# Two root products in three fp32r terms and one weight slab split on VectorE, in a relational graph network

## What is computed

```python
def _rgcn(x, W_rel, W_root, bias, src, dst, etype):
    xr = jnp.einsum('ni,rio->rno', x, W_rel)
    msg = xr[etype, src]
    out = x @ W_root + bias
    for r in range(NUM_RELATIONS):
        m = etype == r
        s = jax.ops.segment_sum(jnp.where(m[:, None], msg, 0.0), dst, num_segments=n)
        c = jax.ops.segment_sum(m.astype(x.dtype), dst, num_segments=n)
        out = out + s / jnp.maximum(c, 1.0)[:, None]
    return out
```

## Time and profile before

| what | value |
|---|---|
| median of three runs | 878.64 us (878.55 to 879.24) |
| the profiled execution, its own time | 879.18 us |
| its span | 877.4 us |
| TensorE matmul busy | 803.3 us, 92% |
| VectorE busy | 604.2 us, 69% |
| ScalarE busy | 388.4 us, 44% |
| GpSimd busy | 502.6 us, 57% |
| mean granted TensorE clock | 0.972 |
| layer 0 about | 60 to 116 us |
| gate of layer 0 | 116 to 283 us |
| layer 1 about | 280 to 345 us |
| layers 2, 3 and 4 about | 516 to 590, 590 to 671, 671 to 755 us |
| attention networks | 755 to 877 us |

### The profile page before, as it was taken

One profiled execution on the slowest core, in us unless ns is written; L12 is line 12 of the kernel. 1 busy time (PEld: TensorE's weight loads), 2 busy tenths in 40 slices (PEclk: granted clock), 3 DMA queues, 4 the chain that ended last, 5 costly groups with the idle time before them and its releaser, 6 DMA issues.

```text
span 877.4 us, 10143 instructions
## 1 busy us (share of the span) xinstructions
PE 803.3 (92%) x4034; PEld 632.5 (72%) x4034; DVE 604.2 (69%) x671; ACT 388.4 (44%) x448; POOL 502.6 (57%) x214
## 2 busy tenths in 40 slices
PE   8999999999788999988997879999999998987987
PEld 3569976775455798666655459987997897864674
DVE  8955149999997622988999968534853888254451
ACT  1124366777663333766765524432342342241521
POOL 0346629999884472899998917661873478000000
PEclk9999999999999999999999989999999999979999
DMA  9036516254332452440533237633652653600000
GB/s 368 2 87 237 160 54 183 61 151 137 108 108 72 164 169 102 133 106 1 204 112 105 72 120 279 212 109 134 226 180 72 247 189 105 237 14 1 1 1 36
DMA packets 24262, 110.98 MB, mean 126 GB/s; under 512 B 3604, under 2 KB 5908, under 8 KB 23832
## 3 DMA queue, kind: packets, MB, share of 16 engines
q1 hardware_dynamic: 23096, 104.24, 36.3%
q10 hardware_dynamic: 1120, 6.10, 1.8%
HBM read 100.63 MB, written 0.79 MB: 116 GB/s over the span
## 4 chain that ended last, share of the span: by engine, by line
PE 61%; DVE 21%; POOL 12%; ACT 4%; issue 2%; DMA 0%; ACTq 0%; DVEq 0%
PE ps L958 22%; DVE prod L1679 12%; PE ps L906 11%; PE ps L943 6%; POOL prod L544 6%; POOL w_lo L532 4%; PE ps L1335 3%; DVE qi_t L1697 3%; PE ps L1195 2%; PE ps L1017 2%; POOL prod L547 2%; PE ps L1038 2%; PE ps L1148 2%; PE ps L1394 2%; PE ps L1320 1%
## 5 line engine op out<-in xcount | busy, mean ns | idle before, releaser
L532 POOL TENSOR_TENSOR w_lo<-w_raw,w_hi 128x1536 fp32r<-128x1536 f32 x54 | 201.5, 3742 | 148.6 <-ACT w_hi L598 148.5
L544 POOL TENSOR_TENSOR prod<-prod 128x1024 f32<-128x1024 f32 x94 | 223.5, 2400 | 49.1 <-DVE prod L1679 48.7
L705 ACT ACTIVATE prod<-ps 128x1024 f32<-128x1024 f32 x192 | 187.1, 1024 | 78.4 <-PE ps L1148 60.5
L1679 DVE TENSOR_TENSOR prod<-prod,ps 128x2048 f32<-128x2048 f32 x96 | 217.6, 2278 | 5.0 <-ACT prod L705 4.0
L1148 PE MATMUL ps<-sel_pair,h_and_q 128*128 128x512 f32 x384 | 129.7, 450 | 24.6 <-ACT prod L705 24.3
L906 PE MATMUL ps<-w_raw,h_t 128*128 128x384 f32 x408 | 141.7, 494 | 0.0
L598 ACT ACTIVATE w_hi<-w_raw 128x1536 fp32r<-128x1536 f32 x54 | 80.3, 1488 | 136.7 <-PE ps L958 92.9
L958 PE MATMUL ps<-w_hi,yt_hi 128*128 128x384 f32 x432 | 111.6, 339 | 8.1 <-POOL w_lo L532 8.1
L906 PEld LDWEIGHTS ps<-w_raw,h_t 128*128 128x128 f32 x408 | 78.7, 194 | 46.6 <-issue 2.6
L1148 PEld LDWEIGHTS ps<-sel_pair,h_and_q 128*128 128x128 f32 x384 | 67.2, 191 | 60.6 <-ACT prod L705 40.4
L958 PE MATMUL ps<-w_lo,yt_hi 128*128 128x384 f32 x432 | 110.4, 336 | 0.0
(11 more groups left out here) (189 smaller groups left out, 1001.8 us busy)
## 6 DMA issues: line engine op xcount, KB each, us to landing
w_raw<-weights SPq DMA_DIRECT2D x105, 768.0 KB, 4.4
wa_in<-weights SPq DMA_DIRECT2D x6, 768.0 KB, 5.8
w_gat<-weights SPq DMA_DIRECT2D x6, 768.0 KB, 8.0
w_query<-weights SPq DMA_DIRECT2D x3, 768.0 KB, 11.2
h_and_q<-stage_hi SPq DMA_DIRECT2D x24, 96.0 KB, 2.1
h_and_q<-stage_lo SPq DMA_DIRECT2D x24, 96.0 KB, 2.2
a_vec<-gat_vectors ACTq DMA_DIRECT2D x1, 2048.0 KB, 8.2
q_t<-queries ACTq DMA_DIRECT2D x1, 1536.0 KB, 10.6
```

The source lines that it names most:

```text
L532: pool.tensor_tensor(Wl[:, j, :], raw_slab(U, 0, j), Wh[:, j, :], ALU.subtract).then_inc(w_lo_ready, 1)
L544: pool.tensor_tensor(v[:, :, 0:32], v[:, :, 0:32], v[:, :, 32:64], ALU.add).then_inc(folded_once, 1)
L705: act.activation(slot_view(s)[:, :, 32 * u:32 * u + 32], args.rearrange("p b (n l) -> p (b n) l", l=LH), ACT.Sigmoid).then_inc(sigmoid_rea ...
L1679: TT(slot_view(s), slot_view(s), ps[:, 6, o:o + L].unsqueeze(1).broadcast_to([P, NB, L]), ALU.mult).then_inc(products_ready, 1)
```

## The change

Five edits, which come together:

1. Layers 3 and 4: the root is a split product in three terms. Its weight slabs get a high part from ScalarE and a low part from VectorE. The turned state is no longer kept in fp32: ScalarE writes its high part (`root_hi`) and VectorE its low part (`root_lo`) from PSUM. Both tiles' roots now run before the first aggregation.
2. All five layers: the low part of the last relation's third slab is written by VectorE, after `relation` of the last relation (in layers 2 to 4 after the `logit_weights` that follows it). GpSimd has the two other slabs and all slabs of the relations before; it has nothing for the roots.
3. Reciprocals of degrees of four types are computed in layer 2 and kept in `rinv4`; layers 3 and 4 compute none (8 fewer on VectorE).
4. ScalarE's list at the change of layer is written anew.
5. On VectorE `counts_of_all` goes from layer 4 to layer 3 (after relation 3), the wait for `vectors_in` behind relation 2 of layer 2, and of the last `logit_weights` the second half goes behind the norm of tile 0.

```diff
-SPLIT = [UNIT[l] + v + 1 for l in range(LAYERS) for v in range(RELATIONS[l])]
+SPLIT = [UNIT[l] + v for l in range(LAYERS) for v in range(l < 3, RELATIONS[l] + 1)]
+ROOTS = [UNIT[l] for l in range(3, LAYERS)]
...
+LO_BY_VECTOR = [(u, 0, j) for u in SPLIT for j in range(3)
+                if u in ROOTS or (j == 2 and u in [UNIT[l] + RELATIONS[l] for l in range(LAYERS)])]
+LO_BY_POOL = [(u, 0, j) for u in SPLIT for j in range(3) if (u, 0, j) not in LO_BY_VECTOR]
...
+            def root_hi(layer, t):
+
+                act.wait_ge(turned[t], layer + 1 if t == 0 else INPUT[layer] + 1)
+                copy(YTh[:, 0, :, t * P:(t + 1) * P], chunk_tile(4 + 2 * t, KC)).then_inc(root_hi_ready[t], 1)
...
                     relu_out(layer, 0)
-                    keep_turned(layer + 3, layer + 2)
+                    w_hi(UNIT[layer + 1], (0,))
+                    root_hi(layer + 1, 0)
+                    h_hi(layer + 1, 0)
+                    w_hi(UNIT[layer + 1], (1,))
+                    relu_out(layer, 1)
+                    w_hi(UNIT[layer + 1], (2,))
+                    h_hi(layer + 1, 1)
+                    root_hi(layer + 1, 1)
                     w_hi(UNIT[layer + 1] + 1, (0,))
-                    h_hi(layer + 1, 0)
-                    relu_out(layer, 1)
-                    h_hi(layer + 1, 1)
...
+            def root_part(layer, t, j):
+
+                if j == 0:
+                    pe.wait_ge(root_lo_ready[t], layer - 2)
+                    root_bias(layer, pair(layer, t))
+                wait_lo(pe, UNIT[layer], j)
+                mm = three_terms(0, j, t, pair(layer, t), False)
+                if t == 1:
+                    mm.then_inc(w_used, 1)
...
                 if layer > 2:
-                    root(layer, 0, 0, 4)
-                if layer in (1, 2):
+                    root_part(layer, 0, 0)
+                    turn(1, e)
+                    root_part(layer, 0, 1)
+                    root_part(layer, 0, 2)
+                elif layer > 0:
...
+                if layer > 2:
+                    for j in range(3):
+                        root_part(layer, 1, j)
...
                 aggregate(layer, 1)
-                root(layer, 1, 4 if degrees is not None else 0, KC)
+                if layer < 3:
+                    root(layer, 1, 4 if degrees is not None else 0, KC)
                 aggregate(layer, 2)
...
+            def w_lo(U, j):
+
+                dve.wait_ge(w_hi_ready, SPLIT_AT[U, 0, j])
+                TT(Wl[:, j, :], raw_slab(U, 0, j), Wh[:, j, :], ALU.subtract).then_inc(w_lo_by_vector, 1)
...
-                dve.reciprocal(rinv[:], deg[:, v - 1, :]).then_inc(rinv_ready, 1)
-                dve.wait_ge(rinv_ready, at_ // 3 + 1)
+                inverse = rinv[:] if layer < 2 else rinv4[:, v - 1, :]
+                if layer < 3:
+                    dve.reciprocal(inverse, deg[:, v - 1, :]).then_inc(rinv_ready, 1)
+                    dve.wait_ge(rinv_ready, at_ // 3 + 1)
...
                     relation(i, v)
+                w_lo(UNIT[i] + RELATIONS[i], 2)
...
                 if layer > 2:
+                    w_lo(UNIT[layer], 0)
+                    root_lo(layer, 0)
                     h_lo(layer, 0)
-                    keep_turned(layer + 2)
+                    w_lo(UNIT[layer], 1)
+                    w_lo(UNIT[layer], 2)
+                    root_lo(layer, 1)
                     h_lo(layer, 1)
...
+                w_lo(UNIT[layer] + RELATIONS[layer], 2)
...
-            logit_weights(0, raw_slab(30, 0, 0), 0, 6, True)
+            logit_weights(0, raw_slab(30, 0, 0), 0, 6, False, (0,))
             last_residual(0)
             norm_shift(2, 0)
+            logit_weights(0, raw_slab(30, 0, 0), 0, 6, True, (1,))
             last_residual(1)
```

77 lines of the change are left out of this document (46 added, 31 removed).

## The result

The change takes 864.07 us (861.38 to 867.81, four runs), against 878.94 us (878.55 to 880.63) for the kernel before: a ratio of 0.9834, 95% interval 0.9804 to 0.9864. That is 14.6 us less, with an interval of 12 to 17 us. Forecast were 865.8 us and 863 to 870. The profiled execution took 861.38 us, its span is 859.5 us; its mean granted clock is 0.983, before it was 0.972.

What follows compares the result with a forecast made beforehand. TensorE's work was taken as the bound, plus the slab GpSimd still owes at each layer's end. Terms 8.0 + 1.7 + 6.0 - 1.4 - 1.5 = 12.8 us off 878.64 gave 865.8 us, range 863 to 870.

Steps and rivals of the forecast that it cites:

- The late third slab: Last relation of each layer: TensorE's waits for GpSimd's slabs go with VectorE's help, 8.0 us saved, bounds 4.2 and 8.1.
- the clock: Layer 4, behind its late slab: without the gap the half clock there goes, 1.7 us saved, bounds 0 and 1.7.
- the rival on a wait that only moves: Layer ends: the split on VectorE moves the wait, to GpSimd's second slab or VectorE's sums; 871.5 us, chance 6%.
- the forecast's sign of no TensorE wait at the end of layers 0 to 3: Ends of layers 0 to 3: TensorE's rows would show no wait for a GpSimd slab.
- VectorE waits for GpSimd and then runs at full speed: Third slab: VectorE starts when GpSimd's slab ends, then takes 1.76 us; in layer 2 in time by half a us.
- The roots: Start of layers 3 and 4: three-term products replace plain ones, 2.99 us saved a layer, 6.0 us for two.
- the uncovered aggregation: Layers 3 and 4: with the root moved, the second aggregation waits for each `yt_lo`, 0.7 us lost a layer, 1.4 together.
- the feed is in time: Roots of layers 3 and 4: ScalarE and VectorE have every part ready, the first by 0.35 us; no wait, bounds 0 to 3.
- The tail: End of layer 4: the moved `logit_weights` half makes tile 1's addition start 1.75 us after its sum; 1.5 us lost.
- the 12% rival: Tail: TensorE idles about 2 us before the logit rows, the clock falls and 3 us of work doubles; 868.8 us, 12%.
- At nothing: Edits priced at zero: eight reciprocals, `counts_of_all` in layer 3, the moved `vectors_in` wait, earlier loads of root and relation slabs.
- The sum: Whole kernel: all terms together take 12.8 us off, giving 865.8 us.

Runs made afterwards that it cites:

- e6: The change with the low parts of the root's slabs in layers 3 and 4 on GpSimd instead of VectorE: 871.01 us, ratio 0.9902.
- e2: The kernel before with only the third slab's low part on VectorE in all layers and the last `w_logit` halves apart; roots plain: 867.86 us, ratio 0.9862.
- e7: The change with the eight reciprocals of layers 3 and 4 computed again: 871.36 us, ratio 0.9906.
- e10: The change with `counts_of_all` at the start of layer 3 and the eight reciprocals of layers 3 and 4 computed again: 867.30 us, ratio 0.9862.
- e12: The kernel before run once more, no edit: 876.87 us in one run.
- e1: The change run again, no edit: 863.40 us, ratio 0.9813 to the kernel before.

## Why the prediction was right

The time was right (865.8 forecast; 864.07 measured, 863.40 in the repetition), the sign too, and 12.8 us lie inside the measured 12 to 17, though below the repetition's 15.0 to 17.9. The mechanism is shown by the rows, which give 12 to 13 us; the 2 to 4 us that the medians gain beyond that were in no term. The range was also narrower than its terms: their bounds, added all one way, reach from 863.6 to 876.8, not from 863 to 868.5. Step by step, against the change's profile:

- *The late third slab, 8.0, and the clock, 1.7.* Right in layers 0, 1, 2 and 4. In the stages: 1.17 us up to the first gate, 0.99 in layer 3 (0.2 between the two repetitions), 5.91 in layer 4, where 1.05, and 1.29 + 2.54 + 1.7 = 5.5 were forecast. In layer 4 nothing of the 1.39 us stayed, and the clock gave 0.3 us more. In layer 3 the wait did not end but changed its slab: 0.34 us in one execution, 1.20 in the other, where the kernel before waited 1.05. That is the rival on a wait that only moves, come true in one layer of five, and the forecast's sign of no TensorE wait at the end of layers 0 to 3 failed there.
- *VectorE waits for GpSimd and then runs at full speed.* Right. In layer 2 GpSimd's slab ends at 568.81 + 4.57 = 573.38, VectorE's at 574.99, 1.61 us later, where the multiply of before had 1.62; TensorE wants it at 575.65. With GpSimd idle, the root's slabs take 1.75 and 1.76 us. (The Trainium skill, SBUF — State Buffer, "SBUF: two separate sides", has the lock concern a VectorE operation in a 2-port perf mode or with two SBUF inputs; the pair of rows of e6, 0.96 us with one in PSUM and 2.81 with both in SBUF, agrees.)
- *The roots, 6.0, and the uncovered aggregation, -1.4.* Net 4.6 forecast, 2.03 + 2.06 = 4.1 found. The roots themselves save 2.95 us a layer, with 2.99 forecast. What was sized too small is the uncovered wait: the two aggregations take 6.66 us, from 598.52 to 605.18, where they took 2.87 + 2.86 = 5.73; that is 0.9 us a layer, not 0.7. That the feed is in time was right to 0.1 us.
- *The tail, -1.5.* Right in mechanism, 1.0 in size: VectorE was ready with the slab earlier, and the addition starts 1.38 us late, not 1.75. The wait of 1.88 us left the clock at full (1.00 from 738 to 742 us), so the 12% rival fell. (The Trainium skill, TensorE: Matmul & The Clock Gate, "What's actually happening", has the clock follow how busy TensorE has been; of the waits named here the one of 1.88 us left it alone, and those of 2.53 and 2.54 us did not.)
- *At nothing.* The total of nothing holds: e2 has neither the reciprocals saved nor the counts moved, and its layers 3 and 4 take the change's time (56.95 and 56.32 us). The reasons given do not hold, and the change's time hides it. `counts_of_all` in layer 3 was put at 3 us in an idle of 9 us; it takes 10.4 us there and fills the idle, because the 3 us were read off a place where GpSimd idles. And "VectorE idles behind them till the sums come" was said of each reciprocal alone: with the counts at their new place the reciprocals would cost 5.5 us (e7), without them 1.4 (e10). So edit 3 makes room for edit 5's move of the counts, and the two together win nothing that e2 lacks. A change with neither of them was not run.
- *The sum.* 10.0 us from Z to T, with 9.7 forecast; 3.0 us in layers 0 to 2, with 3.1 forecast. The rest of the profiled difference is clock. Against the other pair of executions (e12 and e1) the same sums are 9.2 and 2.5 us. What is off in one term (0.3 to 0.9 us) is small beside the sum. The forecast of 865.8 us lies some 2 us above the two medians; that is the part which stands in no term.

## What to carry to other kernels

Take the low part, or any helper's work, to the engine that is free when it is wanted, but count the idle time that covers it once: of several edits "at nothing" that lean on the same idle stretch, each must be priced with the others in place. A VectorE copy, or an operation with two inputs, whose operands all lie in SBUF must be priced at the place where it will stand: beside GpSimd's slabs it took its own time and up to 3.3 us more (3.79 us for 0.49), however small it was, and it can delay the next slab too. And compare two profiles stage by stage, with a repetition of both, before any gain or loss under 2 us is put down to an edit; then hold the sum of the stages against the medians, and say what is left over.
